# The adapters' second factors as matmuls of 64 rows on two halves of the array, and the last expert blocks written by halves

## What is computed

```python
def lora_add(base, inp, A, B):
    Ab = A[layer_idx][lora_indices]
    Bb = B[layer_idx][lora_indices]
    t = jnp.einsum('bri,bni->bnr', Ab, inp)
    return base + jnp.einsum('bor,bnr->bno', Bb, t) * SCALE
gate = lora_add(jnp.einsum('bnh,fh->bnf', x, W_gate), x, A_gate, B_gate)
up = lora_add(jnp.einsum('bnh,fh->bnf', x, W_up), x, A_up, B_up)
act = jax.nn.silu(gate) * up
down = lora_add(jnp.einsum('bnf,hf->bnh', act, W_down), act, A_down, B_down)
...
logits = x @ W_gate + b_gate
_, top_idx = jax.lax.top_k(logits, TOP_K)
y_all = jax.nn.relu(jnp.einsum('bsd,edh->bseh', x, W_e) + b_e)
y = jnp.take_along_axis(y_all, top_idx[..., None], axis=2)
return y.mean(axis=2)
```

## Time and profile before

| | us |
|---|---|
| median of 3 runs | 1826.98 |
| lowest, highest | 1826.32, 1827.26 |
| the profiled execution | 1827.05 |
| its span in the trace | 1825.1 |

### The profile page before, as it was taken

One profiled execution on the slowest core, in us unless ns is written; L12 is line 12 of the kernel. 1 busy time (PEld: TensorE's weight loads), 2 busy tenths in 40 slices (PEclk: granted clock), 3 DMA queues, 4 the chain that ended last, 5 costly groups with the idle time before them and its releaser, 6 DMA issues.

```text
span 1825.1 us, 24866 instructions
## 1 busy us (share of the span) xinstructions
PE 1805.4 (99%) x8400; PEld 1492.5 (82%) x8400; DVE 1248.4 (68%) x1496; ACT 755.6 (41%) x1205; POOL 1093.2 (60%) x712
## 2 busy tenths in 40 slices
PE   9999999999999999999999999999999999999997
PEld 7788888888787888888888888788788888888886
DVE  8977888885568697888888886478688643224400
ACT  5544444444543336444443445443323333333332
POOL 2788888872444445556665553444434777777674
PEclk9999999999999999999999999999999999999999
DMA  6566566645567655555666565577536875567543
GB/s 231 164 235 222 204 205 234 236 144 190 173 249 243 222 187 175 186 179 182 188 214 208 189 201 192 193 264 233 207 120 188 247 194 152 143 184 197 150 104 48
DMA packets 128971, 350.31 MB, mean 192 GB/s; under 512 B 15296, under 2 KB 17216, under 8 KB 128576
## 3 DMA queue, kind: packets, MB, share of 16 engines
q1 hardware_dynamic: 110896, 286.94, 45.9%
q0 software_dynamic: 17952, 61.75, 13.9%
HBM read 267.49 MB, written 90.05 MB: 196 GB/s over the span
## 4 chain that ended last, share of the span: by engine, by line
PE 92%; DVE 2%; DMA 2%; issue 2%; ACT 1%; POOL 1%; SPq 0%; DVEq 0%; POOLq 0%; ACTq 0%
PE PS L1857 28%; PE PS L1858 28%; PE PS L1859 28%; PE PS L1906 2%; PE PS L1987 2%; PE PS L2216 2%; DVE R L1014 1%; DMA raw<-wt_scratch 0%; DVE R L980 0%; DMA ytp<-in_agu,idx_a 0%; PE PS L2056 0%; PE PS L2057 0%; PE PS L2062 0%; PE PS L2128 0%; DVE ring L960 0%
## 5 line engine op out<-in xcount | busy, mean ns | idle before, releaser
L1857 PE MATMUL PS<-R,ring 128*128 128x512 f32 (+1 forms) x1804 | 707.8, 392 | 4.6 <-DVE ring L960 1.4
L1858 PE MATMUL PS<-R,ring 128*128 128x512 f32 (+1 forms) x1804 | 703.1, 390 | 0.0
L1859 PE MATMUL PS<-R,ring 128*128 128x512 f32 (+1 forms) x1804 | 702.5, 389 | 0.0
L1857 PEld LDWEIGHTS PS<-R,ring 128*128 128x128 f32 x1804 | 339.1, 188 | 74.1 <-issue 4.5
L1859 PEld LDWEIGHTS PS<-R,ring 128*128 128x128 f32 x1804 | 338.6, 188 | 71.8
L1858 PEld LDWEIGHTS PS<-R,ring 128*128 128x128 f32 x1804 | 339.1, 188 | 65.4
L828 POOL TENSOR_TENSOR ring<-raw,ring 128x1024 fp32r<-128x1024 f32 x78 | 191.2, 2451 | 266.0 <-ACT ring L967 265.9
L1857 PE MATMUL PS<-ring,R 128*128 128x512 f32 x592 | 231.2, 391 | 1.2 <-DVE FT L1339 1.1
L1859 PE MATMUL PS<-ring,R 128*128 128x512 f32 x592 | 230.5, 389 | 0.0
L1858 PE MATMUL PS<-ring,R 128*128 128x512 f32 x592 | 230.5, 389 | 0.0
L807 POOL DMA_INDIRECT brw<-in_bgu,idx_b x88 | 96.7, 1098 | 222.0 <-DVE R L1149 187.1
(11 more groups left out here) (195 smaller groups left out, 2377.2 us busy)
## 6 DMA issues: line engine op xcount, KB each, us to landing
raw<-in_wp SPq DMA_DIRECT2D x122, 512.0 KB
act_scratch<-FT SPq DMA_DIRECT2D x140, 256.0 KB, 4.8
FT<-act_scratch SPq DMA_DIRECT2D x70, 512.0 KB, 4.3
raw<-in_we SPq DMA_DIRECT2D x64, 512.0 KB
ytp<-in_wgb SPq DMA_DIRECT2D x96, 256.0 KB
raw<-wt_scratch SPq DMA_DIRECT2D x40, 512.0 KB
out<-in_xn SPq DMA_DIRECT2D x17, 512.0 KB, 5.6
y_scratch<-FT SPq DMA_DIRECT2D x7, 1024.0 KB, 6.6
```

The lines of the kernel that those rows point to most:

```text
L1857: e.matmul(out_, hi, whi, start=start, stop=False, skip_group_check=True)
L1858: e.matmul(out_, hi, wlo, start=False, stop=False, skip_group_check=True)
L1859: return e.matmul(out_, lo, whi, start=False, stop=stop, skip_group_check=True)
```

## The change

- The second factors lie over 64 rows for a pair of two halves w: w = 0 in partitions 0 to 63, w = 1 in 64 to 127 (for the second layer it is the two batches instead). The 64 rows are four groups of 16. One gather of 128 rows brings what two gathers of 96 rows brought. DVE's subtraction is two instructions of 16 rows for each one of 32.
- `lora1_out` does the eight matmuls of a pair in a row behind product 6, each 64 rows x 256 columns, alternating between the lower and the upper rows and between banks. Nothing stands behind product 1 any more. The program gives these matmuls a tile of 64 x 128 of the array, where those of 96 rows had the full 128 x 128.
- `lora2_out` likewise: four matmuls of 64 rows x 512 columns, lower and upper rows in turn.
- The first factors have 128 weight columns instead of 64 (a tile of the full array instead of 128 x 64), so T comes out of PSUM with its copies; `ag_hi` and `ad_hi` on ACT write each first factor three times.
- `e_copy` k = 3 gets a tile of its own, the half of `brw` that is free now; all four `c_add` of a pair stand behind product 6. At the start, pair 0's adapter parts stand behind product 3 of pair 1, and its four silus behind them.
- Blocks 31 and later: the first 512 columns get bias, relu and a scatter of their own (`scatter_half`) before the second 512 are ready; the second 512 go through copy, bias and relu in quarters of 256 columns.

```diff
-        TT = R[0:96, TT_O:TT_O + 2048].rearrange("p (w q n) -> p w q n", w=2, q=2)
+        def tt(t, c0, n):
+            b = TT_O + 512 * (1 - t) + c0
+            return R[:, b:b + n]
         def b_t(n):
-            b = BT_O + (n % 2) * 1024
-            return R[0:96, b:b + 1024]
+            b = BT_O + (n % 2) * 512
+            return R[:, b:b + 512]
...
-            for j in range(2):
-                e.indirect_dma_start(out=brw[0:96, j * 512:(j + 1) * 512], out_offset=None,
-                                     in_=bgu.rearrange("(r a) n -> r (a n)", a=2),
-                                     in_offset=ioa(idx_b[0:96, 4 * g + 2 * w + j, p:p + 1])).then_inc(s_br, 16)
+            e.indirect_dma_start(out=brw[:, 0:512], out_offset=None, in_=bgu.rearrange("(r a) n -> r (a n)", a=2),
+                                 in_offset=ioa(idx_b[:, 2 * g + w, p:p + 1])).then_inc(s_br, 16)
...
+            e.wait_ge(s_zc, 2 * b + 1)
+            part(0, 512).then_inc(s_ba0, 1)
+            if b >= LATE:
+                scatter_half(e, b, 0)
+                e.wait_ge(s_zq, b - LATE + 1)
+                part(512, 256).then_inc(s_bq, 1)
+                e.wait_ge(s_zc, 2 * b + 2)
+                part(768, 256).then_inc(s_ba, 1)
...
             for bi in range(4):
-                e.activation(ag_t(bi)[:, :, 0:16], ag_raw(g, bi), ACT.Copy).then_inc(s_gh, 1)
+                v = ag_raw(g, bi).rearrange("p q (o m) -> p q o m", o=1).to_broadcast([128, 16, 3, 16])
+                e.activation(ag_t(bi)[:, :, 0:48].rearrange("p q (o m) -> p q o m", o=3), v, ACT.Copy).then_inc(s_gh, 1)
...
-            elif q and k == 0:
-                e.wait_ge(s_c, c_of(g, q - 1, 2))
-            elif q and k == 1:
-                e.wait_ge(s_c, c_of(g, q - 1, 3))
-            elif k == 3:
-                e.wait_ge(s_c, c_of(g, q, 0))
+            elif q and k < 2:
+                e.wait_ge(s_c, c_of(g, q - 1, 3 * k))
...
-                        act.add(early(48.9 if k == 0 else 52.5 + 0.1 * k), plain_silu, k)
+                        act.add(early(52.5 + 0.1 * k), plain_silu, k)
...
-                    due = op(g, when_at(g, q, [(5 if q == 0 else 4) if q < 2 else 1, 6, 6, 6][k]) + [1.1, 1.05, 1.1, 1.15][k])
+                    due = op(g, when_at(g, q, 6) + [1.04, 1.05, 1.1, 1.15][k])
...
+            e.activation(y[:, 1, 0:256], PS[:, 5 + 2 * (b % 2), 0:256], ACT.Copy).then_inc(s_zq, 1)
+            e.activation(y[:, 1, 256:512], PS[:, 5 + 2 * (b % 2), 256:512], ACT.Copy).then_inc(s_zc, 1)
+            e.wait_ge(s_bq, i + 1)
+            e.activation(y[:, 1, 0:256], y[:, 1, 0:256], ACT.Relu, scale=0.5)
+            e.wait_ge(s_ba, b + 2)
+            e.activation(y[:, 1, 256:512], y[:, 1, 256:512], ACT.Relu, scale=0.5).then_inc(s_zr, 1)
...
-                                m = e.matmul(PS[0:64, 6 + w, cols], R[:, b:b + 64], xc(o, part, k)[:, cols],
+                                m = e.matmul(PS[:, 6 + w, cols], ag_w(2 * w + i, k0 + k), xc(o, part, k)[:, cols],
...
+            def lora1_ready(g, q):
+                e.wait_ge(s_bl, b_val(g, q // 2, q % 2, 1))
+                e.wait_ge(s_t1l, 4 * g + 4)
+
+            def lora1_half(g, q, r, w, bank, i):
+
+                h = rows64(w)
                 t = r if q >= 20 else q % 2
-                e.wait_ge(s_bl, b_val(g, q // 2, q % 2, w))
-                e.wait_ge(s_t1l, 4 * g + 2 * w + 2)
+                o = i * 256 + r * 128
+                return e.matmul(PS[:, bank, i * 256:(i + 1) * 256], b_t(g * 26 + q)[h, o:o + 128], tt(t, i * 256, 256)[h],
+                                start=False, stop=True, skip_group_check=True)
+
+            def lora1_out(g, q, banks):
+
+
+                lora1_ready(g, q)
                 for i in range(2):
-                    cols = slice(i * 256, (i + 1) * 256)
-                    o = (2 * w + i) * 256 + r * 128
-                    m = e.matmul(PS[:, bank, cols], b_t(n)[:, o:o + 128], TT[:, w, t, cols],
-                                 start=False, stop=last and i == 1, skip_group_check=True)
+                    for r in range(2):
+                        for w in range(2):
+                            m = lora1_half(g, q, r, w, banks[2 * w + r], i)
                 return m
...
                     m = main1(g, n, "B21", bk + 1, True)
-                    if q >= 2:
-                        m = lora1_out(g, q, 0, 0, bk + 1)
...
                     main1(g, n, "T4", bk + 3, True)
-                    lora1_out(g, q, 0, 1, bk + 2)
                     e.wait_ge(s_ec, ec + 4)
-                    lora1_out(g, q, 1, 1, bk)
-                    m = lora1_out(g, q, 1, 0, bk + 3)
+                    m = lora1_out(g, q, [bk + 1, bk + 3, bk + 2, bk])
...
-                        m = e.matmul(PS[0:64, 7, :], ad_w(w, c), a_ring(j, part)[:, a * 512:(a + 1) * 512],
+                        m = e.matmul(PS[:, 7, :], ad_w(w, c), a_ring(j, part)[:, a * 512:(a + 1) * 512],
...
+            OUT2 = [0, 2, 1, 3]
...
-                e.matmul(PS[:, bank(s, i), :], TT[:, w, 0, i * 128:(i + 1) * 128], b_t(n)[:, (i // 2) * 512:(i // 2 + 1) * 512],
+                h = rows64(i // 2)
+                e.matmul(PS[:, bank(s, i), :], tt(0, w * 256 + (i % 2) * 128, 128)[h], b_t(n)[h, :],
                          start=False, stop=True, skip_group_check=True).then_inc(s_z, 1)
...
-                    lora1_out(0, 0, 0, 0, 0)
-                    lora1_out(0, 0, 1, 0, 1)
-                    product(0, 1, 0)
-                    product(0, 1, 1)
-                    product(0, 1, 2)
-                    lora1_out(0, 0, 0, 1, 2)
-                    lora1_out(0, 0, 1, 1, 3).then_inc(s_p0, 1)
-                    for j in range(3, 7):
+                    for j in range(4):
+                        product(0, 1, j)
+                    lora1_out(0, 0, [0, 1, 2, 3]).then_inc(s_p0, 1)
+                    for j in range(4, 7):
                         product(0, 1, j)
```

More of the change, by code:

```diff
@@ L814, in gather_d @@
             w, h = divmod(i, 2)
[L815 to L817 removed]
+            e.indirect_dma_start(out=brw[:, 0:512], out_offset=None, in_=bdn,
+                                 in_offset=ioa(idx_d[:, 2 * g + w, h:h + 1])).then_inc(s_br, 16)
         def b_val(g, p, t, w):
@@ L903, in add_bias, with part, scatter_half @@
             off = e.snap(side * 1024) if b >= 2 else 0
-            for n in range(2):
-                e.wait_ge(s_zc, 2 * b + n + 1)
-                z = sbuf2[:, 2 * (b % 2) + n, :]
-                if b >= 2:
-                    bias = AB[:, bass.ds(off + n * 512, 512)]
-                else:
-                    bias = AB[:, n * 512:n * 512 + 512]
-                e.tensor_tensor(z, z, bias, ALU.add).then_inc(s_ba if n else s_ba0, 1)
+            def part(c0, n):
+                z = sbuf2[:, 2 * (b % 2) + c0 // 512, c0 % 512:c0 % 512 + n]
+                bias = AB[:, bass.ds(off + c0, n)] if b >= 2 else AB[:, c0:c0 + n]
+                return e.tensor_tensor(z, z, bias, ALU.add)
+            e.wait_ge(s_zc, 2 * b + 1)
[6 more added lines that the diff above has]
+                part(768, 256).then_inc(s_ba, 1)
+            else:
+                e.wait_ge(s_zc, 2 * b + 2)
+                part(512, 512).then_inc(s_ba, 1)
+        def scatter_half(e, b, n):
+            if n:
+                e.wait_ge(s_zr, b + 1)
+                e.wait_ge(s_sc, 16 * b)
+            else:
+                e.wait_ge(s_z0, b - LATE + 1)
+                e.wait_ge(s_sc, 16 * LATE)
+                if b > LATE:
+                    e.wait_ge(s_sh, 16 * (b - LATE))
+            e.indirect_dma_start(out=out.rearrange("t (a n) -> (t a) n", a=2), out_offset=ioa(sidx2[:, n, b - LATE:b - LATE + 1]),
+                                 in_=sbuf2[:, 2 * (b % 2) + n, :], in_offset=None,
+                                 compute_op=ALU.add).then_inc(s_sc if n else s_sh, 16)
         def scatter(e, b):
+            if b >= LATE:
+                scatter_half(e, b, 1)
+                return
             e.wait_ge(s_zr, b + 1)
@@ L1176, in t2_hi @@
             e.wait_ge(s_t2, n + 1)
-            for r in range(2):
-                for i in range(2):
-                    c = slice(i * 256, (i + 1) * 256)
-                    m = e.activation(TT[32 * r:32 * r + 32, w, 0, c], PS[32 * i:32 * i + 32, 7, c], ACT.Copy, scale=0.5)
-                m.then_inc(s_t2h, 1)
+            for i in range(2):
+                e.activation(tt(0, w * 256, 256)[rows64(i)], PS[rows64(i), 7, i * 256:(i + 1) * 256], ACT.Copy,
+                             scale=0.5).then_inc(s_t2h, 1)
         def t2_lo(e, g, w):
@@ L1938, in product @@
                     m = main1(g, n, "B22", bk + 2, False)
-                    if q < 2 and (g, q) != (1, 0):
-                        m = lora1_out(g, q, 0, 0, bk + 1)
                 elif j == 5:
@@ L2072, in tail2 @@
                 lora2_ready(g, s)
-                for i in range(4):
+                for i in OUT2:
                     lora2_out(g, s, i)
```

190 lines of the change are left out of this document (118 added, 72 removed).

## The result

| | before | after |
|---|---|---|
| median | 1826.91 us (1826.32 to 1827.26, 4 runs) | 1856.17 us (1854.45 to 1859.64, 4 runs) |
| ratio | 1 | 1.0163 (95%: 1.0145 to 1.0180) |
| profiled execution: span, time | 1825.1, 1827.05 us | 1853.5, 1855.31 us |

The change makes the kernel 29 us slower. The prediction was 1801, with a range up to 1820. The tail got 2 us shorter. What else differs lies in three places: the adapter groups, a new wait ahead of them, and the start.

The account below looks back on a forecast made before the run. The kernel was taken as one row of matmuls, bound by PE, idle 19.7 of 1825.1 us. Terms -21.1 - 3.7 + 0.7 + 0.8 - 1.0 - 1.8 = -26.1 took 1827.05 to 1801 us; range 1798.5 to 1820.

Parts of the forecast that it names:

- rival D: At 104 tile changes by rows the array empties, 0.16 to 0.35 us each: 1816.9 (chance 0.04) to 1836.6 us (0.09).
- E: DVE's bunched additions make each of 42 pairs wait 0.3 us, +12.6: 1813.6 us; chance 0.04.
- 3: Visits to the 64 x 128 tiles: 52 at 0.013 us each, +0.7 us.
- 7: Unpriced: fewer gathers, `b_lo` in 16-row pieces beside PE, four bunched `c_add` taking 2.7 us, covered by 2.7 and 8.2.
- 1: `lora1_out`: 352 matmuls become 176 fully overlapping couples of 0.120 us each, -21.1 us.
- B: In the couples, weight loads of the two halves queue up, 0.203 us a couple: 1815.5 us; chance 0.25.
- C: The halves do not overlap, a `lora1_out` couple costs 0.240 us: 1825.8 us, no measurable change; chance 0.08.
- 2: `lora2_out`: 32 matmuls become 16 overlapping couples of 0.232 us, -3.7 us.
- D mild: Each of the 104 tile changes by rows costs 0.16 us, 16.6 in all: 1816.9 us; chance 0.04.
- 4: First factors with 128 weight columns: 128 matmuls cost 0.007 us more each, +0.8 us.
- 5: Start: PE's waits for `b_lo` (0.90 us) and `e_copy` (0.32) go, -1.0 us, bounds -2.3 and +2.
- 6: End: the last scatter starts 0.3 us earlier and its halved transfer takes 1.5 us less, -1.8 us.

Follow-up runs that it names:

- e10: Changed kernel with each group of eight half-array adapter matmuls split into two groups of four, two couples going ahead of T4's last three full matmuls; 1879.75 us in one run.
- e14: e9 with pair 1's first `e_copy` earlier on ScalarE, without the upper rows' four matmuls per group; the remaining four take 0.66 us, kernel time not given.
- e2: Changed kernel with `b_hi` and `b_lo` of w=1 earlier (key 14p+2.6) and `t1_lo` of w=1 back behind the first half of `x0_t3`; 1874.52 us.
- e6: Changed kernel with `b_lo` of t=0, w=1 earlier on VectorE alone (14p+2.1) and `t1_lo` of w=1 back behind the first half of `x0_t3`; 1861.58 us.
- e9: Changed kernel with e7's and e8's edits together and `t1_lo` of w=1 back behind the first half of `x0_t3`; 1820.56 us, 0.9967 of before.
- e7: Changed kernel with one added wait: GpSimd's next mixing is held back until the four `gated` of the pair before are done; 1829.32 us, 1.0007 of before.
- e8: Changed kernel with each pair of 16-row subtractions in `b_lo` and `bd_lo` made one instruction over all 128 rows; 1821.97 us, 0.9972 of before.

## Why the prediction was wrong

It put 0.09 on a slower kernel, and all of that on rival D. The slowdown is none of the rivals as priced: the cost of a change of tile (D) is real but only takes away a gain, and the loss is of E's kind, VectorE's list too late for PE, at another place and with another size. Two steps failed: the price of a visit by rows (3), and the list of VectorE put at no price (7). By number as in the prediction:

1. *Couples.* Right: 0.117 us a couple against 0.120, by e10, and e14 shows that the two halves overlap. Rivals B (0.203) and C (0.240) are false.
2. *`lora2_out`.* 8 x (0.86 - 0.93) is -0.6 us instead of -3.7, by the visits again.
3. *Changes of tile.* The step that failed in the sum. I took 0.013 us a visit from the row of a column split, and it is 0.40 by rows: 52 visits are 21 us instead of 0.7. That takes away most of the 24.8 us of terms 1 and 2. The range had this as D mild (0.16 a change; it is 0.20) with a chance of 0.04; the row was of another kind of split, and did not hold for this one.
4. *Wider first factors.* Right in size: 32 of them take 3.83 us, 3.63 before, so 128 cost 0.8 more. No wait for `ag_hi`.
5. *Start.* The 0.90 wait at 38.59 is gone as foreseen, but the end of pair 1 comes 3.1 us later, beyond my bound of +2. What came late next was not the list before T4's lo part but `e_copy`, behind a ScalarE list that waited for `t1_lo`'s move on VectorE. I had not followed that moved key. It explains about 2.1 us of the wait (e2, e6); in e9 the larger part of what is left is `b_hi` waiting for its gather, with `e_copy` behind it.
6. *End.* -1.8 foreseen; the distance from the last matmul to the end is 9.2 us, 2.1 less than before. The last scatter starts 0.3 us earlier, as foreseen, and the part behind its start is 1.8 shorter, for 1.5.
7. *"Without a price".* The step that cost the sign. I wrote that `b_lo` becomes 16-row pieces "beside PE", and gave the bunched `c_add` a cover of 2.7 and 8.2 us against the next pair. I did not ask what stands behind them on VectorE: `gated` four at a time, and behind that the `b_lo` on which the group now depends. Nor did I count instructions: 88 `b_lo` became 176. The trace of the kernel before would have shown the margin, had I compared the end of the `b_lo` that is needed with the start of the group:

```profile
795.36 1.67 DVE L1149 TENSOR_TENSOR R<-brw,R 32x512 fp32r<-32x512 f32 x1
797.65 0.88 PE L1906 MATMUL PS<-R 96*128 96x256 f32 x6
```

That is 0.6 us, and it is 0.6 in eight even pairs of the second pass. In the first pass it is 1.2 once and 2.4 us and more otherwise, and the changed kernel waits there for up to 3.6: the list grew by more than those margins too. What this cost: 27.3 us of waits and some 3.8 of slow clock behind them, against 12.6 in rival E, at a chance of 0.04.

The sum with the measured terms, by the profiled executions: -4.4 for 44 groups, -0.6 for 8 groups of the second layer, +0.4 for the first factors of the second pass, +27.3, +3.8, +3.1 at the start, -2.1 at the end: +27.5. The spans differ by 28.4; the 0.9 left is a balance of small waits, on `e_copy` (1.0 in two) and `w_lo` (0.7) among others, against some that only the kernel before had. I did not test these.

With 0.40 us a visit the prediction's -26.1 becomes -6.0, and e9, where the waits ahead of the adapters are gone, gains 7 us on the kernel before. That the two are so near is in part luck: e9 still waits 3.5 us at its start, where the prediction had a gain of 1.0.

Of the two causes of the late list, the moved `gated` beside GpSimd and the doubled `b_lo`, each can be taken away alone and the loss goes (e7, e8). So neither is "the" cause, and how the 27 us divide between them has no answer.

## What to carry to other kernels

Price moved and added instructions on every engine by count, and for each compare the end of the last one that somebody waits for with the start of that somebody in the old trace: a margin of 0.6 us, repeated pair after pair, belongs in the sum, and so does one of 3 us where the list grows by more, even on an engine that is 80% busy. If moving one item in a late list only changes who waits, shorten the list. A measured cost of one kind of tile change says nothing on another kind; gather half-array matmuls into as few groups as the banks allow, and expect nothing from a group under four couples of this size (four save 0.48 us, and the visit costs 0.40).
